# A spectral convolution whose three output blocks share one block product, with the even lags and the odd lags taken in turn

## The chip, the cores and the metric

The kernel runs on one core of a Trainium2 chip. The metric is the device time of one execution in microseconds (us), the median of the runs of a kernel. PE is the matmul engine TensorE and PEld its weight loads, DVE is VectorE, ACT is ScalarE, POOL is GpSimd and SP is SyncE, whose queue issues the loads used here.

## The reference, cut to what matters

The whole kernel is a small network of four blocks. The change touches one part, the spectral unit (`_L0_ffn_ref` in the reference). For 16 filters `phi[:, k]` of 4096 taps it makes the causal convolution of the tokens `u` with the filter and with its sign-alternated twin, and multiplies each result by a 128x128 matrix of that filter:

```
Vf = rfft(phi); Uf_p = rfft(u); Uf_m = rfft(u * sgn)
U_plus  = irfft(Vf * Uf_p)[:sl]
U_minus = irfft(Vf * Uf_m)[:sl] * sgn
out  = einsum('btkd,k,kde->bte', U_plus, sigma**0.25, Mpp)
out += einsum('btkd,k,kde->bte', U_minus, sigma**0.25, Mpm)
```

The plus and minus results are the sum and the difference of the convolution over the even lags and that over the odd lags. So the kernel computes these two instead, and mixes them with `Mpp + Mpm` and `Mpp - Mpm`. The output is added over four prefixes of the sequence, each with its own matrices and weight, which is why a mixing product is cut at 144, 288, 576 and 1152 positions.

## The kernel before, in words

Here there are 4 sequences (`B`) of 2304 tokens. Tokens are split by parity, so each sequence has 1152 (`HALF`) positions in each of two parities `q`. They are cut into 9 blocks (`GB`) of 128 for the inputs and into 3 ranges `c` (`NCW`) of 384 (`CW`) for the outputs. A causal convolution is then a lower triangular block matrix: output range `c` is a sum over the input blocks up to it. Three input blocks against one output range are a **block product**: nine matmuls of 384 columns where the lags are full, and three each of 384, 256 and 128 columns on the diagonal, where half the square is empty. There are three matmuls for each block because every operand is kept as a rounded high half and a low half, of which three of the four products are made.

`spectral_unit` normalises and transposes the tokens, `autoregress` makes a short convolution into `YT` and splits the tokens into `u_high` and `u_low`, and `convolve` does the work of this study. In `convolve`, for each filter `k` of 16 (`NK`), 24 units `(b, c, q)` are run with `c` from 2 down to 0. For a unit:

- TensorE's `conv` (L1068) makes the even lags into one bank of PSUM and the odd lags into the next: 3 block products for each kind where `c` is 2, 2 where it is 1, 1 where it is 0, one of which is the diagonal one.
- ScalarE (L1107) copies both banks as `uk_high`; VectorE (`lower`, L1163) subtracts this copy from the banks and so makes `uk_low`. Both work on 128x768.
- TensorE's `mix` (L1084), two units behind `conv`, multiplies by the matrices into bank 6 or 7, both kinds into one sum; VectorE adds it to `YT` (L1175, 128x384).

GpSimd splits the filters of the next `k` into halves (L1122, L1124: four operations of 1152 elements), kept twice. SyncE loads filters and matrices. VectorE prepares the next matrices in seven steps. The order is that of the code on each engine, held together by semaphores; TensorE's loop body (L1049) holds two filters, so it jumps back seven times. At the end of each filter TensorE waits for its own last `mix` before it releases the filters:

```
for n in range(UNITS):
    conv(n)
    if n >= 2:
        mix(n - 2)
mix(UNITS - 2)
mix(UNITS - 1)
pe.wait_ge(s["mixed"], k * UNITS + (UNITS + 3))
pe.sem_inc(s["filter_used"], 1)
```

## Time and profile before

| what | value |
|---|---|
| median of three runs | 11514.84 us (11510.84 to 11519.92) |
| the profiled execution, its device time | 11517.94 us |
| its span, first to last instruction | 11515.4 us |
| mean granted TensorE clock over the span | 0.884 |
| busy over the whole span | PE 81%, DVE 57%, ACT 38%, POOL 34% |
| `convolve`, first matmul to last addition | 4627.15 to 7406.71 us, 2779.6 us |

The shares over the whole span mix many stages. `convolve` is one of them, a quarter of the time, and its rows are read by themselves. A matmul row shows when it starts and how long it takes to the end of its pipeline; neighbours overlap, so the cost of one is the distance from its start to the next start. A row of waits says which engine stood idle, and what ended that.

### The profile page before, as it was taken

The page shows a single profiled execution, that of the slowest core. Times are in us where ns is not written, and L with a number is a line of the kernel's source. Part 1 is how long each engine was busy: PE and PEld are TensorE (multiplying, and loading weights), DVE is VectorE, ACT ScalarE, POOL GpSimd, SP SyncE. Part 2 cuts the span into 40 slices and gives each one's busy share as a digit, 9 for nine tenths or more (in the row PEclk, how much of TensorE's full clock was granted, in tenths as well). Part 3 has the DMA queues.
Part 4 walks back from the last instruction along what each step waited for, and adds up shares of the span by engine and source line. Part 5 has one row for each costly group of instructions (what it writes and reads, how often), then busy time and mean ns, then how long its engine had stood idle before and what let it go on. Part 6 is the DMA issues. An engine that isn't in the chain of part 4 may idle for free. (4 is left out here: it accounts for less than half of the span.)

```text
span 11515.4 us, 138604 instructions
## 1 busy us (share of the span) xinstructions
PE 9299.0 (81%) x45020; PEld 6323.7 (55%) x45020; DVE 6604.9 (57%) x8044; ACT 4361.7 (38%) x7821; POOL 3888.3 (34%) x2670
## 2 busy tenths in 40 slices
PE   4777777777777775999999999778748989897567
PEld 2334343333433343999999999767523333333355
DVE  6999799899979995222222222211256566652446
ACT  4666566556646664111111111122313444444221
POOL 4998699689959993100000000000000000000001
PEclk8888888898888888999999999866858999998677
DMA  3454355344535452000000000111210100001110
GB/s 124 155 159 140 123 155 159 116 147 156 158 95 167 157 157 65 25 13 7 13 13 7 13 13 1 50 45 30 118 35 20 23 17 13 17 13 63 66 27 17
DMA packets 335211, 831.37 MB, mean 72 GB/s; under 512 B 37778, under 2 KB 111894, under 8 KB 324060
## 3 DMA queue, kind: packets, MB, share of 16 engines
q1 hardware_dynamic: 334628, 823.93, 23.1%
q8 instruction: 325, 5.32, 0.2%
q14 instruction: 258, 2.11, 0.1%
HBM read 757.40 MB, written 37.82 MB: 69 GB/s over the span
## 5 line engine op out<-in xcount | busy, mean ns | idle before, releaser
L669 POOL TENSOR_TENSOR ss_work<-ss_dtu,ss_ringb 128x768 f32<-128x768 f32 x1536 | 2754.1, 1816 | 3.8
L557 PE MATMUL ss_ps<-ss_work,ss_ident 128*128 128x512 f32 (+1 forms) x6144 | 2369.2, 538 | 264.3 <-DVE ss_work L640 158.5
L557 PEld LDWEIGHTS ss_ps<-ss_work,ss_ident 128*128 128x128 f32 x6144 | 1247.2, 210 | 1165.2 <-issue 761.0
L653 DVE TENSOR_TENSOR_SCAN ss_work<-ss_ps,ss_last,ss_work 128x768 f32<-128x768 f32 x1024 | 1801.1, 1797 | 0.0
L1163 DVE TENSOR_TENSOR cv_uk_low<-cv_ps,cv_uk_high 128x768 fp32r<-128x768 f32 x384 | 367.7, 958 | 2086.8 <-ACT cv_uk_high L1107 2086.8
L582 ACT ACTIVATE ss_ps<-ss_dt,ss_a_neg 128x768 f32<-128x768 f32 x1536 | 1370.5, 892 | 174.0 <-DVE ss_work L653 166.9
L1107 ACT ACTIVATE cv_uk_high<-cv_ps 128x768 fp32r<-128x768 f32 x384 | 311.9, 812 | 2480.6 <-PE cv_ps L1068 2480.6
L640 DVE TENSOR_TENSOR ss_work<-ss_work,ss_ps 128x1280 f32<-128x1280 f32 x768 | 1126.6, 1467 | 134.2 <-ACT ss_ps L582 114.8
L2142 DVE TENSOR_REDUCE at_top<-at_ps 128x384 f32 (+1 forms) x1728 | 888.7, 551 | 259.1 <-PE at_ps L2061 258.1
L2124 ACT ACTIVATE at_probs<-at_ps 128x768 f32<-128x768 f32 x864 | 695.9, 810 | 872.1 <-PE at_ps L2078 872.1
L653 DVE TENSOR_TENSOR_SCAN ss_work<-ss_ps,ss_work 128x768 f32<-128x768 f32 x512 | 871.0, 1737 | 64.2 <-POOL ss_work L669 64.1
L1122 POOL TENSOR_TENSOR cv_even_high<-cv_even,cv_one 128x1152 fp32r<-128x1152 f32 x16 | 33.7, 2106 | 2307.2 <-PEq L1096 2294.2
L1068 PE MATMUL cv_ps<-cv_even_high,stu_u_high 128*128 128x384 f32 (+2 forms) x2304 | 737.3, 320 | 52.4 <-issue 29.7
L1543 POOL MEMSET c_pooled<- 128x2048 f32 x2 | 3.6, 1807 | 2283.5 <-POOLq L59 2283.5
L2078 PE MATMUL at_ps<-at_packs 128*128 (+1 forms) x3456 | 711.3, 332 | 76.1 <-PEq L59 58.4
L2085 PE MATMUL at_ps<-at_probs,at_v 128*64 128x384 f32 x3456 | 753.4, 515 | 15.6 <-ACT at_probs L2124 13.5
L1068 PE MATMUL cv_ps<-cv_even_low,stu_u_high 128*128 128x384 f32 (+2 forms) x2304 | 744.2, 323 | 0.0
L1068 PE MATMUL cv_ps<-cv_even_high,stu_u_low 128*128 128x384 f32 (+2 forms) x2304 | 741.2, 322 | 0.0
L529 PE MATMUL ss_ps<-ss_dtr,ss_dtw 64*128 64x192 f32 (+1 forms) x736 | 294.6, 489 | 548.3 <-DVE ss_work L640 519.6
L1068 PE MATMUL cv_ps<-cv_odd_low,stu_u_high 128*128 128x384 f32 (+2 forms) x2304 | 736.4, 320 | 0.0
L1068 PE MATMUL cv_ps<-cv_odd_high,stu_u_high 128*128 128x384 f32 (+2 forms) x2304 | 736.3, 320 | 0.0
L1068 PE MATMUL cv_ps<-cv_odd_high,stu_u_low 128*128 128x384 f32 (+2 forms) x2304 | 735.7, 319 | 0.0
(527 smaller groups left out, 15405.1 us busy)
## 6 DMA issues: line engine op xcount, KB each, us to landing
ss_ringb<-scan_rows SPq DMA_DIRECT2D x768, 384.0 KB, 3.7
ss_ringc<-scan_rows SPq DMA_DIRECT2D x768, 384.0 KB, 3.8
c_w<-in_l_ffn_w SPq DMA_DIRECT2D x64, 1024.0 KB, 7.0
at_packs<-at_parts SPq DMA_DIRECT2D x192, 144.0 KB, 3.2
cv_odd<-in_l_ffn_phi_odd SPq DMA_DIRECT2D x16, 576.5 KB, 5.7
cv_even<-in_l_ffn_phi_even SPq DMA_DIRECT2D x16, 576.0 KB, 4.1
ffa_rows<-rows SPq DMA_DIRECT2D x16, 576.0 KB, 6.3
ffb_w<-in_l_conv_fw SPq DMA_DIRECT2D x50, 128.0 KB, 2.0
```

The costliest lines, as they stand in the source:

```text
L557: ins = pe.matmul(acc[:, d * WIN + a:d * WIN + e], ident[:, :], weighed[:, t % DEEP, d, a:e], start=False, stop=n == NST - 1, skip_group_c ...
L582: act.activation(decay[d], dt[:, i % 2, d, :], ACT.Exp, scale=a_neg[:, SECTIONS[i][0], d, n:n + 1]).then_inc(s["decayed"], 1)
L640: dve.tensor_tensor(weighed[:, t % DEEP, :, 0:SPLIT], hid[:, t % DEEP, :, 0:SPLIT], bc(spread_c[:, None, :], [P, D2, SPLIT]), ALU.mult).th ...
L653: dve.tensor_tensor_scan(hid[:, t % DEEP, d, ::step], decay[d][:, ::step], drive[:, t % DEEP, d, ::step], start, ALU.mult, ALU.add).then_i ...
L669: pool.tensor_tensor(drive[:, t % DEEP, d, :], dtu[:, t // NST % 2, d, :], ringb[:, t % RING, :], ALU.mult).then_inc(s["driven"], 1)
L1068: ins = pe.matmul(ps[:, 2 * (n % 3) + kind, off:CW], (u_high, u_low)[a][:, b * GB + g, parity, :], filters[f][:, u, ::-1][:, from_:from_ + ...
L1107: act.activation(uk_high[:, n % 3, :, :], ps[:, at:at + 2, 0:CW], ACT.Copy).then_inc(s["kept"], 1)
L1163: dve.tensor_tensor(uk_low[:, n % 3, :, :], ps[:, at:at + 2, 0:CW], uk_high[:, n % 3, :, :], ALU.subtract).then_inc(s["lowered"], 1)
L2078: ins = pe.matmul(ps_bank(ps, 2 * (j % 2) + h)[:, 0:R], packs[:, pair, k, h, j * P:(j + 1) * P], packs[:, pair, q, h, bass.ds(c * R, R)], ...
L2085: ins = pe.matmul(acc[64 * h:64 * h + 64, 0:R], v[:, j, 2 * pair + h, :, :].rearrange("p a d -> p (a d)"), probs[:, j % 3, h, :], start=j ...
L2124: act.activation(probs[:, j % 3, :, :], ps[:, 2 * (j % 2):2 * (j % 2) + 2, 0:R], ACT.Exp).then_inc(s["weighed"], 1)
L2142: dve.tensor_reduce(top[:, bass.ds(tile + h * NT_, 1), u], ps_bank(ps, 5 + u % 3)[:, 0:R], AX.X, ALU.max).then_inc(s["reduced"], 1)
```

## The change

Write the block matrix with `F0` for the diagonal block of taps, `F1` and `F2` for the next ones, and `u0`, `u1`, `u2` for the three ranges of input. The outputs are `F0 u0`, `F1 u0 + F0 u1` and `F2 u0 + F1 u1 + F0 u2`: three diagonal products and three full ones. The new code makes one product `F1 (u0 + u1)` (`SHARED`), `F0 u0` (`FIRST`), `(F0 - F1) u1` (`SECOND`) and `(F2 - F1) u0 + F0 u2` (`THIRD`), and VectorE adds the shared product to the second and third output (`join`). That is two diagonal products and four bank groups with three full ones: one diagonal product fewer, five block products in place of six.

The even and the odd kind are run in turn: a filter is now 16 units (`PER`) `(kind, b, q)`, first all eight even ones. The banks are 0 to 3 for the four products and 4 to 6 for the mixing of `c` 0, 1 and 2. Each kind is mixed and added to `YT` by itself. The taps `near` (F0 and F1), `less` (F0 - F1) and `far` (F2 - F1) of a kind are kept once and made by GpSimd from one raw tile in nine operations for each kind. `autoregress` also makes the sums `u0 + u1` and splits them (`s_high`, `s_low`). TensorE's loop body holds one filter, the first filter stands ahead of the loop.

```
+            s_high, s_low = (flat[:, i * n:(i + 1) * n].rearrange("p (g t c) -> p g t c", t=2, c=C).bitcast(F32R) for i in range(2))
+            spare = flat[:, 2 * n:3 * n].rearrange("p (s t) -> p s t", t=CW).bitcast(F32R)
...
+                for b in range(B):
+                    dve.tensor_tensor(sums[:, b], U[:, b * GB:b * GB + NCW, :, :], U[:, b * GB + NCW:b * GB + 2 * NCW, :, :], ALU.add).then_inc(s["summed"], 1)
...
+                for b in range(B):
+                    dve.wait_ge(s["sum_cut"], b + 1)
+                    dve.tensor_tensor(s_low[:, b * NCW:(b + 1) * NCW, :, :], sums[:, b], s_high[:, b * NCW:(b + 1) * NCW, :, :], ALU.subtract)
...
+                    act.wait_ge(s["summed"], b + 1)
+                    act.activation(s_high[:, b * NCW:(b + 1) * NCW, :, :], sums[:, b], ACT.Copy).then_inc(s["sum_cut"], 1)
...
+    PAIRS = [(b, q) for b in range(B) for q in range(2)]
+    PER = 2 * len(PAIRS)
...
+        raw = sb("raw", [P, HALF + 1])
+        near = [[sbr(f"near{kind}{part}", [P, WIDE + kind]) for part in range(2)] for kind in range(2)]
+        less = [[sbr(f"less{kind}{part}", [P, APART + kind]) for part in range(2)] for kind in range(2)]
+        far = [[sbr(f"far{kind}{part}", [P, APART + kind]) for part in range(2)] for kind in range(2)]
+        apart = sb("apart", [P, APART + 1])
...
+        shared = sb("shared", [P, 2, CW])
...
+                with sp.Fori(0, NK) as k:
+                    sp.wait_ge(ready[1], k + 1)
+                    sp.dma_start(raw[:, 0:HALF], bass.AP(w["phi_even"].tensor, k * rows, [[1, P], [1, HALF]])).then_inc(loaded[0], 16)
...
+                    sp.wait_ge(ready[0], k + 2)
+                    sp.dma_start(raw[:, :], bass.AP(w["phi_odd"].tensor, k * rows, [[1, P], [1, HALF + 1]])).then_inc(loaded[1], 16)
...
+                        pool.wait_ge(loaded[kind], k * 16 + 16)
+                        pool.wait_ge(s["convolved"], k * (4 * PER) + 2 * PER * (kind + 1))
+                        halve(1, near[kind], taps[:, CW:HALF + kind], WIDE + kind)
+                        pool.tensor_tensor(apart[:, 0:CW + kind], taps[:, WIDE:WIDE + CW + kind], taps[:, CW:WIDE + kind], ALU.subtract).then_inc(s["split"], 1)
+                        pool.tensor_tensor(apart[:, CW + kind:more], bc(none[:, :], [P, 2 * P]), taps[:, WIDE + kind:WIDE + 2 * P + kind], ALU.subtract).then_inc(s["split"], 1)
+                        pool.wait_ge(s["split"], done + 3)
+                        halve(4, less[kind], apart[:, 0:more], more).then_inc(s["split"], 1)
+                        pool.wait_ge(s["split"], done + 5)
+                        pool.tensor_tensor(apart[:, 0:more], taps[:, 0:more], taps[:, CW:CW + more], ALU.subtract).then_inc(s["split"], 1)
+                        pool.wait_ge(s["split"], done + 6)
+                        halve(7, far[kind], apart[:, 0:more], more).then_inc(ready[kind], 1)
...
+                def product(n, bank, blocks, taps, first, narrow, start, stop):
+                    kind, b, q = unit(n)
+                    parity, shift = ((q, 0), (1 - q, q))[kind]
+                    for g in range(NCW):
+                        off = g * P if narrow else 0
+                        from_ = first + shift - (0 if narrow else g * P)
+                        for turn, (a, f) in enumerate(HI_LO):
+                            ins = pe.matmul(ps[:, bank, off:CW], blocks(a, g, parity), taps[kind][f][:, ::-1][:, from_:from_ + CW - off],
+                                            start=start and g == 0 and turn == 0, stop=stop and g == NCW - 1 and turn == 2, skip_group_check=True)
+                    return ins
...
+                    at = k * (NCW * PER) + (NCW * n + c + 1)
+                    pe.wait_ge(s["kept"], at)
+                    pe.wait_ge(s["lowered"], at + NCW)
+                    pe.wait_ge(s["added"], at)
+                    for lo, hi, seg in pieces(c):
+                        for turn, (a, f) in enumerate(HI_LO):
+                            ins = pe.matmul(ps[:, 4 + c, lo:hi], (eff_high, eff_low)[a][:, kind, seg, :], (uk_high, uk_low)[f][:, (NCW * n + c) % SLOTS, lo:hi],
+                                            start=turn == 0, stop=turn == 2, skip_group_check=True)
+                    ins.then_inc(s["mixed"], 1)
+
+                def body(k, before):
+                    for n in range(PER):
+                        kind, b, q = unit(n)
+                        if n % len(PAIRS) == 0:
+                            pe.wait_ge(ready[kind], k + 2)
+                        last = k * (NCW * PER) + NCW * n
+                        pe.wait_ge(s["shared"], k * PER + (n + 1))
+                        product(n, SHARED, lambda a, g, parity: (s_high, s_low)[a][:, b * NCW + g, parity, :], near, CW, False, True, True).then_inc(s["convolved"], 1)
+                        if n or before is not None:
+                            mix(k if n else before, n - 1 if n else PER - 1, 0)
+                        pe.wait_ge(s["lowered"], last + 1)
+                        product(n, FIRST, of(b, 0), near, 0, True, True, True).then_inc(s["convolved"], 1)
+                        if n or before is not None:
+                            mix(k if n else before, n - 1 if n else PER - 1, 1)
+                        pe.wait_ge(s["lowered"], last + 2)
+                        product(n, SECOND, of(b, 1), less, 2 * P, False, True, True).then_inc(s["convolved"], 1)
+                        if n or before is not None:
+                            mix(k if n else before, n - 1 if n else PER - 1, 2)
+                        pe.wait_ge(s["lowered"], last + 3)
+                        product(n, THIRD, of(b, 0), far, 2 * P, False, True, False)
+                        product(n, THIRD, of(b, 2), near, 0, True, False, True).then_inc(s["convolved"], 1)
+
+                pe.sem_inc(s["convolved"], 4 * PER)
+                body(0, None)
+                with pe.Fori(0, NK - 1) as i:
+                    body(i + 1, i)
...
+                        act.wait_ge(s["convolved"], made + SHARED + 1)
+                        act.wait_ge(s["joined"], k * (2 * PER) + (2 * n + 2))
+                        act.activation(shared[:, n % 2, :], ps[:, SHARED, 0:CW], ACT.Copy).then_inc(s["shared"], 1)
+                        for c in range(NCW):
+                            if c:
+                                act.wait_ge(s["joined"], k * (2 * PER) + (2 * n + c + 4))
+                            else:
+                                act.wait_ge(s["convolved"], made + FIRST + 1)
+                            act.wait_ge(s["mixed"], free + c + 1)
+                            act.activation(uk_high[:, (NCW * n + c) % SLOTS, :], ps[:, FIRST + c, 0:CW], ACT.Copy).then_inc(s["kept"], 1)
...
+                    dve.tensor_tensor(ps[:, FIRST + c, 0:CW], ps[:, FIRST + c, 0:CW], shared[:, n % 2, :], ALU.add).then_inc(s["joined"], 1)
+
+                def body(k, before, after):
+                    for n in range(PER):
+                        late = (k, n - 1) if n else (before, PER - 1)
+                        for c in range(NCW):
+                            if late[0] is not None:
+                                add(*late, c)
+                            if c:
+                                join(k, n, c)
+                            lower(k, n, c)
+                        if n in (2, 3):
+                            halve_matrices(n - 2, 1, k * (NCW * PER) + SLOTS)
+                        if after is not None and 9 <= n < 14:
+                            sum_matrices(n - 9, after)
+                        if after is not None and n >= 14:
+                            halve_matrices(n - 14, 0, k * (NCW * PER) + (SLOTS + NCW * PER // 2))
```

On TensorE, this stood in the middle of a filter before, the end of the even lags of a unit with `c` = 2 and the start of its odd lags (`stu_u_high` is the weight, `cv_even_high` the moving taps):

```order
L1068 MATMUL cv_ps<-cv_even_high,stu_u_high 128x256
L1068 MATMUL cv_ps<-cv_even_low,stu_u_high 128x256
L1068 MATMUL cv_ps<-cv_even_high,stu_u_low 128x256
L1068 MATMUL cv_ps<-cv_even_high,stu_u_high 128x128
L1068 MATMUL cv_ps<-cv_even_low,stu_u_high 128x128
L1068 MATMUL cv_ps<-cv_even_high,stu_u_low 128x128
L1068 MATMUL cv_ps<-cv_odd_high,stu_u_high 128x384
L1068 MATMUL cv_ps<-cv_odd_low,stu_u_high 128x384
L1068 MATMUL cv_ps<-cv_odd_high,stu_u_low 128x384
```

Now the first filter's second unit begins like this (`stu_XT` holds `s_high` and `s_low` in the shared product and `uk_high` and `uk_low` in the mixing one):

```order
L1103 MATMUL cv_ps<-cv_near,stu_XT 128x384 [waits cv_shared]
L1103 MATMUL cv_ps<-cv_near,stu_XT 128x384 x8
L1120 MATMUL cv_ps<-stu_XT,cv_eff_high 128x144 [waits cv_lowered,cv_added,cv_kept,cv_eff_ready]
L1120 MATMUL cv_ps<-stu_XT,cv_eff_high 128x144
L1120 MATMUL cv_ps<-stu_XT,cv_eff_low 128x144
L1120 MATMUL cv_ps<-stu_XT,cv_eff_high 128x144 x2
L1120 MATMUL cv_ps<-stu_XT,cv_eff_low 128x144
L1120 MATMUL cv_ps<-stu_XT,cv_eff_high 128x96 x2
L1120 MATMUL cv_ps<-stu_XT,cv_eff_low 128x96
L1103 MATMUL cv_ps<-cv_near,stu_u_high 128x384 [waits cv_lowered]
L1103 MATMUL cv_ps<-cv_near,stu_u_high 128x384
```

The shared product stands first in a unit, and the mixing of the unit before is spread behind the four products, one range at a time, with a wait ahead of each. A diagonal group (384, 256, 128 columns) is what there is one fewer of. At the end of TensorE's loop body the rows are these:

```order
L1103 MATMUL cv_ps<-cv_near,stu_u_low 128x128
L1148 REGISTER_ALU
L1148 COMPARE_AND_BRANCH
L1120 MATMUL cv_ps<-stu_XT,cv_eff_high 128x144 [waits cv_added,cv_lowered,cv_kept]
```

The jump stands behind each filter and no wait for TensorE's own `mix` is ahead of it; the last row is the first one after the loop.

On VectorE, in the middle of a filter before, the subtractions of 768 elements and the additions to `YT` alternate:

```order
L1163 TENSOR_TENSOR cv_uk_low<-cv_ps,cv_uk_high 128x768 [waits cv_kept]
L1175 TENSOR_TENSOR stu_YT<-stu_YT,cv_ps 128x384 [waits cv_mixed]
L1161 REGISTER_ALU
L1163 TENSOR_TENSOR cv_uk_low<-cv_ps,cv_uk_high 128x768 [waits cv_kept]
L1175 TENSOR_TENSOR stu_YT<-stu_YT,cv_ps 128x384 [waits cv_mixed]
L1161 REGISTER_ALU
L1163 TENSOR_TENSOR cv_uk_low<-cv_ps,cv_uk_high 128x768 [waits cv_kept]
```

And now (L1206 adds to `YT`, L1216 is `join`, L1210 is `lower`):

```order
L1206 TENSOR_TENSOR stu_YT<-stu_YT,cv_ps 128x384 [waits cv_mixed]
L1216 TENSOR_TENSOR cv_ps<-cv_ps,cv_shared 128x384 [waits cv_convolved,cv_shared]
L1210 TENSOR_TENSOR stu_XT<-cv_ps,stu_XT 128x384 [waits cv_kept]
L1206 TENSOR_TENSOR stu_YT<-stu_YT,cv_ps 128x384 [waits cv_mixed]
L1216 TENSOR_TENSOR cv_ps<-cv_ps,cv_shared 128x384 [waits cv_convolved]
L1210 TENSOR_TENSOR stu_XT<-cv_ps,stu_XT 128x384 [waits cv_kept]
L1206 TENSOR_TENSOR stu_YT<-stu_YT,cv_ps 128x384 [waits cv_mixed]
L1210 TENSOR_TENSOR stu_XT<-cv_ps,stu_XT 128x384 [waits cv_kept]
```

The eight rows are one unit: three additions, two joins and three subtractions, all of 384 elements. A filter has 16 such units, 128 operations; before it had 24 pairs, 48 operations. An addition, which waits for TensorE's mixing, now stands ahead of each subtraction or join, which release a bank.

## Rows read from the trace of the kernel before

**Rows 1.** Windows of two stretches: busy time and instructions by engine, granted clock, DMA share, GB/s

```profile
4650.00:4824.00 174.00, 173.50 (x1176) 173.40 (x1175) 40.16 (x61) 20.31 (x25) 9.47 (x4) 1.00 0.04 11
4824.00:4998.00 174.00, 169.59 (x1135) 169.50 (x1134) 39.23 (x60) 18.68 (x23) 9.01 (x4) 0.98 0.04 11
```

**Rows 2.** Waits from 4600 to 7420: us in total, times, longest us

```profile
ACT cv_uk_high L1107 <- PE cv_ps L1068: 2480.6, 384, 28.8
PE cv_ps L1068 <- issue: 29.7, 7, 4.4
PE cv_ps L1068 <- POOL cv_odd_low L1124: 18.7, 1, 18.7
PE cv_ps L1068 <- PE cv_ps L1084: 4.0, 8, 0.5
```

**Rows 3.** Timeline of TensorE at 5007: start us, us, what

```profile
5007.62 0.34 PE L1068 MATMUL cv_ps<-cv_even_high,stu_u_low 128*128 128x384 f32 x1
5007.79 0.28 PE L1068 MATMUL cv_ps<-cv_even_high,stu_u_high 128*128 128x256 f32 x1
...
5008.15 0.23 PE L1068 MATMUL cv_ps<-cv_even_high,stu_u_high 128*128 128x128 f32 x1
...
5008.43 0.39 PE L1068 MATMUL cv_ps<-cv_odd_high,stu_u_high 128*128 128x384 f32 x1
5008.66 0.34 PE L1068 MATMUL cv_ps<-cv_odd_low,stu_u_high 128*128 128x384 f32 x1
```

**Rows 4.** Timeline of ScalarE: first and last of seven copies

```profile
5205.16 0.81 ACT L1107 ACTIVATE cv_uk_high<-cv_ps 128x768 fp32r<-128x768 f32 x1 [10.00 <-PE cv_ps L1068]
...
5247.74 0.81 ACT L1107 ACTIVATE cv_uk_high<-cv_ps 128x768 fp32r<-128x768 f32 x1 [10.00 <-PE cv_ps L1068]
```

**Rows 5.** Timeline of GpSimd: the first operation of three filters

```profile
4798.90 2.11 POOL L1122 TENSOR_TENSOR cv_even_high<-cv_even,cv_one 128x1152 fp32r<-128x1152 f32 x1 [156.31 <-PEq L1096]
...
4969.88 2.11 POOL L1122 TENSOR_TENSOR cv_even_high<-cv_even,cv_one 128x1152 fp32r<-128x1152 f32 x1 [161.36 <-PEq L1096]
...
5146.41 2.11 POOL L1122 TENSOR_TENSOR cv_even_high<-cv_even,cv_one 128x1152 fp32r<-128x1152 f32 x1 [167.36 <-PEq L1096]
```

**Rows 6.** Timeline of TensorE where its loop jumps back

```profile
4969.43 0.28 PE L1084 MATMUL cv_ps<-cv_uk_high,cv_eff_low 128*128 128x96 f32 x1
4974.11 0.66 PE L1068 MATMUL cv_ps<-cv_even_high,stu_u_high 128*128 128x384 f32 x1 [4.41 <-issue]
...
4979.04 0.34 PE L1068 MATMUL cv_ps<-cv_even_high,stu_u_high 128*128 128x384 f32 x1
```

**Rows 7.** Groups of VectorE by line and form, 4600 to 7420

```profile
L1163 DVE TENSOR_TENSOR cv_uk_low<-cv_ps,cv_uk_high 128x768 fp32r<-128x768 f32 x384 | 367.7, 958 | 2086.8 <-ACT cv_uk_high L1107 2086.8
L1175 DVE TENSOR_TENSOR stu_YT<-stu_YT,cv_ps 128x384 f32<-128x384 f32 x384 | 210.0, 547 | 59.0 <-PE cv_ps L1084 58.8
```

**Rows 8.** Timeline around the start of the stage

```profile
4608.57 0.49 ACT L999 ACTIVATE stu_YT<-ar_ps 128x384 f32 x1 [1.45 <-PE ar_ps L987]
...
4616.53 2.11 POOL L1122 TENSOR_TENSOR cv_even_high<-cv_even,cv_one 128x1152 fp32r<-128x1152 f32 x1 [6.50 <-DMA cv_odd<-in_l_ffn_phi_odd]
...
4619.10 3.09 DVE L1141 TENSOR_TENSOR cv_mm<-cv_mp,cv_mm 128x512 f32<-128x512 f32 x1
...
4627.15 0.66 PE L1068 MATMUL cv_ps<-cv_even_high,stu_u_high 128*128 128x384 f32 x1 [18.71 <-POOL cv_odd_low L1124]
```

**Rows 9.** Timeline: VectorE while GpSimd works, some us later

```profile
4638.18 2.10 POOL L1122 TENSOR_TENSOR cv_odd_high<-cv_odd,cv_one 128x1153 fp32r<-128x1153 f32 x1
...
4638.70 0.96 DVE L1163 TENSOR_TENSOR cv_uk_low<-cv_ps,cv_uk_high 128x768 fp32r<-128x768 f32 x1 [8.09 <-ACT cv_uk_high L1107]
```

**Rows 10.** Timeline of ScalarE and VectorE at the end of the stage

```profile
7400.80 0.81 ACT L1107 ACTIVATE cv_uk_high<-cv_ps 128x768 fp32r<-128x768 f32 x1 [2.97 <-PE cv_ps L1068]
...
7406.15 0.56 DVE L1175 TENSOR_TENSOR stu_YT<-stu_YT,cv_ps 128x384 f32<-128x384 f32 x1 [1.46 <-PE cv_ps L1084]
```

**Rows 11.** Timeline of VectorE in `autoregress`

```profile
4562.56 4.96 DVE L971 TENSOR_TENSOR stu_u_low<-stu_u,stu_u_high 128x4608 fp32r<-128x4608 f32 x1 [5.45 <-ACT stu_u_high L994]
```

More of the change, by code:

```diff
@@ L1189, in convolve @@
+                ch.leave(NK - 2)
+                body(NK - 1, NK - 2, None)
+                for c in range(NCW):
+                    add(NK - 1, PER - 1, c)
         s.end()
```

245 lines of the change are left out of this document (104 added, 141 removed).

## The prediction

> **What bounds the kernel now.** I read the windows first. In a stretch of one filter TensorE is busy 173.50 of 174 us at a granted clock of 1.00, VectorE 40.16, ScalarE 20.31 and GpSimd 9.47 [rows 1]. The waits say the same from the other side: ScalarE waits for TensorE 384 times, 2480.6 us in all, while TensorE's own waits in the stage are 18.7 us for the first filters, seven of together 29.7 us put down to nothing that the profile shows, and eight of together 4.0 us for its own mixing [rows 2]. So TensorE's stream of matmuls sets the time of the stage; the other engines cost nothing until they hold it up.
>
> The price of a matmul is read from the distance of starts. Full ones of 384 columns follow each other at 0.17 to 0.18 us. A diagonal group's 256s begin at 5007.79 and its 128s at 5008.15, and the next group starts at 5008.43; the matmul after that follows at 0.23 us instead of 0.175, a price of a short group that goes to whoever stands behind it [rows 3]. One round of six units, both kinds of one `(b, q)`, is 5247.74 - 5205.16 = 42.58 us for two, 21.29 us for one [rows 4]. Eight of them are 170.3 us. Filters follow at 4969.88 - 4798.90 = 170.98 us where no loop jump lies between, and at 5146.41 - 4969.88 = 176.53 us where one does [rows 5]. The jump itself is seen: the last mixing matmul starts at 4969.43, the next at 4974.11, with 4.41 us idle for "issue", and then 15 matmuls take 4979.04 - 4974.11 = 4.93 us, 0.32 us each where 0.175 was usual [rows 6]. That is TensorE at the lower level of its clock, 1.2 GHz, after it stood still for 4.4 us. So a jump costs about 4.5 us of standing and 4.93 - 15 x 0.175 = 2.3 us of slow matmuls, 6.8 us; the two periods give 176.53 - 170.3 = 6.2 us. I take 6.5. The end of a filter without a jump costs 170.98 - 170.3 = 0.7 us, the wait for its own mixing.
>
> **TensorE's work.** For each kind and `(b, q)` one diagonal product goes: three matmuls of 384 (3 x 0.175 = 0.53 us) and six shorter ones (5008.43 - 5007.79 = 0.64 us), together 1.17 us [rows 3]. The penalty of 0.05 us behind a short group does not go, since a unit now has three places where a long group follows a short one and two old units of one kind had about as many. There are 16 filters x 8 x 2 = 256 such products: 256 x 1.17 = 299.5 us less. The mixing has the same matmuls as before, in other order. A unit of one kind is then (21.29 - 2.34) / 2 = 9.48 us, a filter 151.6 us. TensorE changes to another group with waits 14 times where it did 12 times for the same work. Such changes are hardly seen: summed from the starts a round is 21.0 us against 21.29 measured, 0.02 us a change. 2 x 0.02 x 128 = 5 us more.
>
> **The loop.** The body holds one filter, and the first filter stands ahead of the loop. 15 passes jump back 14 times, before 7. Before: 7 x 6.5 + 8 x 0.7 = 51 us. After: 14 x 6.5 = 91 us, with no wait for the own mixing. That is 40 us more. The body is 1008 matmuls with as many loads where it was 2304; if it is still fetched anew at each jump, the price of a jump stands. Bounds for a jump: nothing, if the shorter body is held (14 x 6.5 = 91 us less than I say), and twice the price, if the other engines' jumps delay the filter's beginning as well (91 us more). The Trainium skill, "Runtime: NRT & Kernel Launch", section "Instruction fetch mechanics", says that a taken branch to a target outside the sequencer's present window forces a fetch before the engine goes on, and gives TensorE's instruction memory as 2048 instructions. The rule speaks against this change, as the trace's seven stops do; by the memory's figure the new body of some 2,090 instructions is just too long to be held, and the sum stays.
>
> **The other engines.** ScalarE copied 128x768 at 0.81 us [rows 4]; 128x384 out of PSUM takes it 0.49 us [rows 8]. A unit of 9.48 us has four such copies, 2.0 us. VectorE took 0.958 us for 768 elements and 0.547 us for 384 [rows 7]; `join`, which writes PSUM, is in no row, and I bound it by 0.547 us (its count of elements) and 0.958 us (twice that) and take 0.55, since both known forms read PSUM and go by the element. Eight operations are 4.4 us, 5.2 at the upper bound, of 9.48; matrix steps add at most 1.5. In TensorE's own order, with 0 the start of a unit: the shared product ends at 1.6, the first at 3.8, the second at 6.1, the third at 9.4. ScalarE has the shared sum by 2.2. The first range is copied and lowered by 5.0, the second joined, copied and lowered by 7.9, the third by 2.0 of the next unit. TensorE wants them for mixing at 1.6, 3.8 and 6.1 of the next unit, and wants the banks again at 2.6, 4.5 and 6.6. The tightest of these is late only if it slips by 4 us or more. Behind an addition on VectorE, which waits for mixing, stand a join and a subtraction; the mixing it waits for is done before the product that they need. So all of this is hidden behind matmuls, at no cost. Where the loop jumps, ScalarE and VectorE jump too, each after its last operation, 1 to 3 us later than TensorE; TensorE's first shared product after a jump ends 7 us after the last third product, and a jump of some 4.5 us on them fits.
>
> GpSimd takes 2.11 us for 1152 elements, 1.83 ns each; at the start, beside VectorE, its four operations took 4627.15 - 4616.53 = 10.6 us for 4610 elements [rows 8]. A kind now has 5376 elements, so 10 to 12.5 us, with a load of some 6.5 us [rows 8] ahead. It has eight units, 75 us, for it. Hidden; if that cover were gone it would cost 19 us for each of 31 kinds.
>
> **The ends.** At the start GpSimd needs to wait only for the even load, up to 2 us sooner, and has up to 2 us more to do before TensorE begins: 0. In `autoregress` VectorE stands idle for 5.45 us ahead of L971 [rows 11], and the four sums of 768 elements, at 4.96 / 4608 us for one, 0.8 us each, fit there. Behind the last copy to `YT`, at 4608.57 [rows 8], ScalarE has four copies of 768 elements more and VectorE a last subtraction: 4 x 0.81 + 0.96 = 4.2 us on the path. At the end, the last copy starts at 7400.80 and the last addition at 7406.15 [rows 10], 5.9 us with it. Now two of the three mixings run while the last range is evicted: join 0.55, copy 0.49, lower 0.55, three matmuls 0.6, addition 0.55, 2.8 us with the handing over 3.2. That is 2.7 us less.
>
> **The sum.** -299.5 + 5 + 40 + 4.2 - 2.7 = -253 us. From the profiled execution's own time, 11517.94, that is 11265; the median of the three runs is 3.1 us lower, so I say 11262 us, 2.2% faster. Three runs of before lie within 9 us, under 0.1%; 0.2% (23 us) is about what can be told from no change.
>
> **The rivals.** *The jumps cost nothing.* The new body is less than half the old. For: loops of few instructions elsewhere need not be fetched. Against: 4.4 us is lost at every one of the seven old jumps [rows 2], and the new body is still over 2000 instructions with its loads. Time: 11262 - 91 = 11171. Chance 0.05.
>
> *The jumps cost twice.* ScalarE's and VectorE's bodies are longer than before in ScalarE's case (64 operations for 24), and the shared sum must be copied before the next shared product may overwrite its bank. Against: the slack of some 3 us at the jump, worked out above. Time: 11262 + 91 = 11353. Chance 0.08.
>
> *VectorE becomes the bound, slower than before.* All three evictions of a unit and its additions pass through VectorE in one fixed order, with GpSimd more than twice as busy beside it. For: with GpSimd at work VectorE took 3.09 us for 512 elements at the start [rows 8]. Against: some 20 us later a subtraction that reads PSUM took 0.96 us beside GpSimd, its usual time [rows 9], and every operation of the unit's chain reads PSUM. It decides from 9.48 us of VectorE's work in a unit, and the kernel is slower than before from 9.48 + 253 / 256 = 10.5 us, 1.3 us an operation. At 1.53 us, half of the 3.09 us row, it is 12.2 us: 256 x (12.2 - 9.48) = 700 us more, 11960. Chance 0.03.
>
> *The single filter buffers are late.* Load and splitting shown at each change of kind, 31 x 19 = 590 us more, 11850. Against: 75 us of cover. Chance 0.02.
>
> *The change does less than it says.* This cannot be by count: the code has 1008 matmuls for a filter in place of 1152. The price of what goes can be smaller: by columns alone, 3 x 768 at 0.175 / 384 us, a product is 1.05 us, and the gain 31 us less. That lies in the forecast's own range.
>
> **How the numbers follow.** The forecast has 0.82. Its own range is 11235 to 11305: the product between 1.05 us (+31) and 1.22 us with the penalty behind it (-13), the jump between 6.2 and 6.8 us (2 us either way), 10 us for the ends. For 8 in 10 I go from 11190, towards the free jumps, to 11360, which holds the doubled ones. Faster by over 0.2%: the forecast and both cases of the jump, 0.94 of their 0.95. Slower: 0.05. Within: 0.01.
>
> **What would show it.** TensorE over 99% busy between jumps, a filter at 151 to 153 us without the jump; 14 waits of 4 to 4.5 us for "issue" and none above 0.5 us for VectorE or ScalarE; `join` at 0.5 to 0.6 us; VectorE near 70 to 75 us busy in a filter, GpSimd 20 to 25; the stage at about 2522 us in place of 2779.6. The prediction is wrong if TensorE waits for `lowered`, `shared` or the filters, if its clock falls between jumps, or if the jumps' price is another.

## The result and the profile after

| | before | after |
|---|---|---|
| median of the runs | 11512.84 us (11507.78 to 11519.92, 4 runs) | 11186.64 us (11167.34 to 11189.08, 4 runs) |
| profiled execution, device time | 11517.94 us | 11187.02 us |
| stage, first matmul to last addition | 2779.6 us | 2426.7 us |
| the rest of that execution | 8738.4 us | 8760.3 us |
| mean granted clock | 0.884 | 0.881 |

The ratio is 0.9713 with a 95% interval of 0.9696 to 0.9729: 2.9% faster, where 2.2% was forecast. The time lies 3 us below the predicted range (11190 to 11360 us). The stage gave 352.9 us, and 257 were forecast for it. The rest of the program took 22 us more in this execution. Some 5 of these are the change's own, 4.5 at the longer end of `autoregress` and 0.8 between it and the first matmul; the others are what the rest varies by, since over the profiled executions of this study it lies between 8727 and 8763 us.

One filter of the changed kernel in the windows, against [rows 1] (same columns):

```profile
4866.00:5017.60 151.60, 150.62 (x1010) 150.48 (x1010) 75.15 (x142) 31.48 (x64) 24.50 (x18) 1.00 0.04 12
```

TensorE is full but for 0.98 us, in a stretch that holds a loop jump. VectorE's 75 us, ScalarE's 31 and GpSimd's 24.5 are what was forecast (70 to 75, 32, and 20 to 25). The waits of the stage, against [rows 2]:

```profile
POOL cv_near L1078 <- PE cv_ps L1103: 1887.1, 30, 63.6
ACT stu_XT L1169 <- DVE cv_ps L1216: 1331.2, 512, 2.8
ACT stu_XT L1169 <- PE cv_ps L1103: 447.9, 256, 1.8
DVE cv_ps L1216 <- PE cv_ps L1103: 446.3, 512, 1.1
PE cv_ps L1103 <- POOL cv_far L1080: 24.0, 1, 24.0
PE cv_ps L1103 <- issue: 14.0, 14, 1.3
```

No row has TensorE waiting for VectorE or ScalarE. Its fourteen jumps cost 14.0 us together, where the seven of before cost 29.7; GpSimd waits 63 us for each kind's turn, so its cover is large. The jump on TensorE, against [rows 6]:

```profile
4941.10 0.27 PE L1103 MATMUL cv_ps<-cv_near,stu_u_low 128*128 128x128 f32 x1
4942.36 1.84 PE L1103 MATMUL cv_ps<-cv_near,stu_XT 128*128 128x384 f32 x9 [0.98 <-issue]
4944.04 0.34 PE L1120 MATMUL cv_ps<-stu_XT,cv_eff_high 128*128 128x144 f32 x2
```

It stands still for 0.98 us, not 4.41, and the nine matmuls behind take 4944.04 - 4942.36 = 1.68 us, 0.187 each: the clock stays at 2.4 GHz. GpSimd's first operation of each filter, against [rows 5], gives the price:

```profile
4715.75 1.47 POOL L1078 TENSOR_TENSOR cv_near<-cv_raw,cv_one 128x768 fp32r<-128x768 f32 x1 [59.27 <-PE cv_ps L1103]
...
4866.12 1.47 POOL L1078 TENSOR_TENSOR cv_near<-cv_raw,cv_one 128x768 fp32r<-128x768 f32 x1 [62.10 <-PE cv_ps L1103]
...
5017.69 1.47 POOL L1078 TENSOR_TENSOR cv_near<-cv_raw,cv_one 128x768 fp32r<-128x768 f32 x1 [63.29 <-PE cv_ps L1103]
```

From the written-out filter into the loop there is no jump: 150.37 us, 9.40 us a unit. With one it is 151.57, and 151.4 to 151.8 over all of them. A jump costs 1.2 us. The groups of the chain, against [rows 7]:

```profile
L1210 DVE TENSOR_TENSOR stu_XT<-cv_ps,stu_XT 128x384 fp32r<-128x384 f32 x768 | 428.2, 558 | 636.8 <-ACT stu_XT L1169 636.8
L1206 DVE TENSOR_TENSOR stu_YT<-stu_YT,cv_ps 128x384 f32<-128x384 f32 x768 | 420.3, 547 | 145.3 <-PE cv_ps L1120 135.5 <-DVE cv_eff_low L1199 8.1
L1169 ACT ACTIVATE stu_XT<-cv_ps 128x384 fp32r<-128x384 f32 x768 | 377.7, 492 | 1779.1 <-DVE cv_ps L1216 1331.2 <-PE cv_ps L1103 447.9
L1216 DVE TENSOR_TENSOR cv_ps<-cv_ps,cv_shared 128x384 f32<-128x384 f32 x512 | 290.1, 567 | 446.3 <-PE cv_ps L1103 446.3
```

`join` takes 567 ns: writing PSUM costs VectorE hardly more than writing `YT`. The ends, against [rows 8, 10]:

```profile
4616.37 0.49 ACT L1010 ACTIVATE stu_YT<-ar_ps 128x384 f32 x1 [1.45 <-PE ar_ps L998]
4616.76 3.03 ACT L1013 ACTIVATE stu_XT<-ar_sums 128x768 fp32r<-128x768 f32 x4
...
4622.20 0.10 POOL L1066 MEMSET cv_one<- 128x1 f32 x1 [37.09 <-POOLq L59]
...
4627.04 1.47 POOL L1078 TENSOR_TENSOR cv_near<-cv_raw,cv_one 128x768 fp32r<-128x768 f32 x1 [4.71 <-DMA cv_raw<-in_l_ffn_phi_even]
...
4628.97 2.28 DVE L1180 TENSOR_TENSOR cv_mm<-cv_mp,cv_mm 128x512 f32<-128x512 f32 x1
```

The four copies of the sums follow the last copy to `YT`, as foreseen. At the other end the last `join` starts at 7063.75, and the last three additions end 3.2 us later:

```profile
7063.75 0.57 DVE L1216 TENSOR_TENSOR cv_ps<-cv_ps,cv_shared 128x384 f32<-128x384 f32 x1 [0.97 <-PE cv_ps L1103]
...
7065.43 1.54 DVE L1206 TENSOR_TENSOR stu_YT<-stu_YT,cv_ps 128x384 f32<-128x384 f32 x3
```

### The profile page after: what moved, and what is told of

Its sections match the earlier page's. It is cut to its first block and busy times, and to the rows that moved or that the text cites. A ratio compares the mean times of both kernels' runs of the same rounds, so it can differ in the third digit from the quotient of the medians.

```text
span 11185.2 us, 139472 instructions
## 1 busy us (share of the span) xinstructions
PE 8980.1 (80%) x42716; PEld 6002.8 (54%) x42716; DVE 7179.1 (64%) x9364; ACT 4559.6 (41%) x8465; POOL 4134.1 (37%) x2895
## 5 line engine op out<-in xcount | busy, mean ns | idle before, releaser
L1169 ACT ACTIVATE stu_XT<-cv_ps 128x384 fp32r<-128x384 f32 x768 | 377.7, 492 | 1779.1 <-DVE cv_ps L1216 1331.2
L1210 DVE TENSOR_TENSOR stu_XT<-cv_ps,stu_XT 128x384 fp32r<-128x384 f32 x768 | 428.2, 558 | 636.8 <-ACT stu_XT L1169 636.8
L1078 POOL TENSOR_TENSOR cv_near<-cv_raw,cv_one 128x768 fp32r<-128x768 f32 (+1 forms) x32 | 46.9, 1467 | 1895.6 <-PE cv_ps L1103 1887.1
L676 POOL TENSOR_TENSOR ss_work<-ss_work,ss_ringc 128x256 f32<-128x256 f32 x768 | 562.2, 732 | 239.1 <-DVE ss_work L653 229.1
L1103 PE MATMUL cv_ps<-cv_near,stu_u_high 128*128 128x384 f32 (+2 forms) x3072 | 635.0, 296 | 0.0
L529 PEld LDWEIGHTS ss_ps<-ss_dtr,ss_dtw 64*128 64x128 f32 x736 | 121.8, 205 | 860.0 <-DVE ss_work L640 769.6
L1120 PE MATMUL cv_ps<-stu_XT,cv_eff_high 128*128 128x144 f32 (+3 forms) x3072 | 577.4, 282 | 0.2 <-issue 0.2
L1216 DVE TENSOR_TENSOR cv_ps<-cv_ps,cv_shared 128x384 f32<-128x384 f32 x512 | 290.1, 567 | 446.3 <-PE cv_ps L1103 446.3
L591 ACT ACTIVATE ss_ps<-ss_ringc 128x512 f32<-128x512 f32 x768 | 461.7, 601 | 253.7 <-DVE ss_work L640 210.9
```

Source lines behind the costliest of these rows:

```text
L676: pool.tensor_tensor(weighed[:, t % DEEP, :, SPLIT:WIN], hid[:, t % DEEP, :, SPLIT:WIN], bc(ringc[:, t % RING, None, SPLIT:WIN], [P, D2, W ...
L1103: ins = pe.matmul(ps[:, bank, off:CW], blocks(a, g, parity), taps[kind][f][:, ::-1][:, from_:from_ + CW - off], start=start and g == 0 and ...
L1120: ins = pe.matmul(ps[:, 4 + c, lo:hi], (eff_high, eff_low)[a][:, kind, seg, :], (uk_high, uk_low)[f][:, (NCW * n + c) % SLOTS, lo:hi], sta ...
```

## The experiments

The question was why a jump now costs 1.2 us and not 6.5. **Theory A:** the jump still brings in code (a fetch), but TensorE issues ahead of its array, and matmuls already issued cover most of the fetch. Before, the wait for its own last mixing emptied the array first (a drain), so the whole fetch was seen, and the pause drew the clock down. **Rival B:** the shorter body is held or fetched faster. Further kernels test the price of a product, of the reordering, and the slack of VectorE. Stages are read from each kernel's profiled execution; medians of kernels that ran together stand beside the kernel before on the same chip.

**Before, without the wait.** The other engines are released by counts of `convolved` in place of `filter_used`.

```
-                        pe.wait_ge(s["mixed"], k * UNITS + (UNITS + 3))
-                        pe.sem_inc(s["filter_used"], 1)
...
-                        pool.wait_ge(s["filter_used"], k + 1)
+                        pool.wait_ge(s["convolved"], k * UNITS + 1)
```

> The kernel before, with one edit: TensorE no longer waits for its own last mixing matmul at the end of a filter; GpSimd takes the release of a filter's buffers from the count of finished convolutions instead, and VectorE has it from its waits for mixing. The loop body is as long as before (2304 matmuls). Theory A (TensorE's sequencer runs ahead of the array and reaches the jump early, so that most of the fetch behind a jump lies under matmuls that are still queued; the wait at the end of a filter took that lead away): the idle time at each of the 7 jumps falls from 4.4 us to about 1 us, the matmuls behind it keep the full clock, and the kernel takes 7 x 5.3 + 8 x 0.7 = 43 us less than before, about 11470 us. Theory B (the jump is cheap in the changed kernel because its loop body is less than half as long): the 7 jumps still cost 4.4 us of idle time and 2.3 us of slow matmuls, only some 10 us are saved, about 11502 us.

11490.99 us (9 runs), ratio to before 0.9971 (0.9961 to 0.9981); stage 2754.2, 25 us less. TensorE at one of its jumps:

```profile
4974.48 0.28 PE L1084 MATMUL cv_ps<-cv_uk_high,cv_eff_low 128*128 128x96 f32 x1
4976.72 0.41 PE L1068 MATMUL cv_ps<-cv_even_high,stu_u_high 128*128 128x384 f32 x1 [1.97 <-issue]
...
4977.95 0.52 PE L1068 MATMUL cv_ps<-cv_even_high,stu_u_high 128*128 128x384 f32 x1
4978.27 0.52 PE L1068 MATMUL cv_ps<-cv_even_low,stu_u_high 128*128 128x384 f32 x1
...
4981.15 0.34 PE L1068 MATMUL cv_ps<-cv_even_low,stu_u_high 128*128 128x384 f32 x1
```

The long body is as it was, and the idle time falls from 4.41 to 1.97 us, and to between 1.62 and 1.89 us at the six other jumps. But the clock still fell: here 1.2 us after the resume, for ten matmuls at 0.32 us (4977.95 to 4981.15), at the six others from the first matmul on, fifteen of them in 4.94 us. A filter with a jump takes 173.4 to 174.4 us against 170.35 without, so a jump still costs 3.0 to 4.1 us, 3.8 in the mean. With the wait it costs 6.3 by the same measure (176.4 to 177.0 us). So here the wait was 2.5 us of the price, all of it standing still; the slow matmuls stayed. Theory A had promised more, 43 us, than the 25 that came, and rival B, with 4.4 us idle as before, fits no better.

**After, with a wait put in** at the end of the body, for the last product of the filter.

```
+                    pe.wait_ge(s["convolved"], k * (4 * PER) + 8 * PER)
```

> The changed kernel, with one wait added: at the end of each filter TensorE waits for its own last product, ahead of the jump. The loop body keeps its length (1008 matmuls). Theory A (the lead of the sequencer hides the fetch): each of the 14 jumps shows some 4 us of idle time, the matmuls after it run at the lower level of the clock for some us, and the kernel is 14 x 5.3 = 74 us slower than the changed one, about 11261 us. Theory B (the short body makes the jump cheap): the wait costs only the emptying of the array, 15 x 0.3 = 5 us, about 11192 us.

11255.69 us (4 runs), 0.9769 (0.9753 to 0.9786); stage 2502.2, 75.5 us more. TensorE at a jump:

```profile
4931.79 0.27 PE L1103 MATMUL cv_ps<-cv_near,stu_u_low 128*128 128x128 f32 x1
4936.27 3.25 PE L1103 MATMUL cv_ps<-cv_near,stu_XT 128*128 128x384 f32 x9 [4.21 <-issue]
4939.32 0.42 PE L1120 MATMUL cv_ps<-stu_XT,cv_eff_high 128*128 128x144 f32 x2
```

With the same short body, 4.21 us of idleness and nine matmuls at 0.34 us are back. All 14 jumps stand 3.7 to 4.2 us, and filters with a jump take 155.9 to 158.4 us, 157.0 in the mean, 6.6 more than the 150.37 without wait and jump. This is the jump that I had priced at 6.5. Theory A holds; rival B had put the whole wait at 5 us. That the median comes within 7 us of my forecast for the changed kernel is in part luck: the stage is 20 us shorter than the 2522 that I had, and the rest of the program longer.

**After, two filters in TensorE's body.** Two filters stand ahead of the loop, and it jumps six times.

```
+                body(1, 0)
+                with pe.Fori(0, NK // 2 - 1) as i:
+                    body(i * 2 + 2, i * 2 + 1)
+                    body(i * 2 + 3, i * 2 + 2)
```

> The changed kernel with two filters in TensorE's loop body (2016 matmuls) and two ahead of the loop: 6 jumps in place of 14. Theory A (lead of the sequencer): a jump costs the same 1.2 us, so 8 x 1.2 = 10 us less, about 11177 us, hardly to be told from the changed kernel. Theory B (length of the body): the jumps get dear again, 6 x 6.5 - 14 x 1.2 = 22 us more, about 11209 us, with idle times near 4 us at the jumps.

11165.58 us (4 runs), 0.9696 (0.968 to 0.9712); stage 2416.8, 9.9 us less. Each of the six jumps costs what the fourteen did:

```profile
PE cv_ps L1103 <- issue: 5.9, 6, 1.3
```

A body of 2016 matmuls jumps as cheaply as one of 1008. Rival B is out between these lengths; that of before is 2304.

**The fetch itself** can be seen in the DMA view of the same traces. The code comes in packets of 16384 bytes on queue 8. In the kernel without any jump of TensorE (its loop written out, below) they follow each other at 16 to 21 us through the stage, though the other engines still jump there. At each jump of TensorE further ones come between. These are the DMA rows of three views of 8 us in 40 slices of 0.2 us, each of which begins 3.0 us ahead of the start of the last matmul before the jump, which is thus at the border of the 15th and the 16th slice. The kernels are the changed one (4938.10 to 4946.10), before without the wait (4971.48 to 4979.48) and the changed one with a wait (4928.79 to 4936.79):

```profile
GB/s 0 0 0 0 0 0 0 82 0 0 0 0 0 0 0 0 0 0 0 0 0 0 0 82 0 0 0 0 0 0 0 0 0 0 0 0 0 0 0 0
GB/s 0 0 0 0 0 0 0 0 0 0 0 82 0 0 0 0 0 0 0 0 0 0 0 0 0 0 0 0 0 82 0 0 0 0 0 0 0 0 0 0
GB/s 0 0 0 0 0 0 0 0 0 0 0 0 0 0 0 0 0 0 0 0 0 0 82 0 0 0 0 0 0 0 0 0 0 0 0 0 0 0 0 82
```

Over all jumps of five kernels, by the packets' starts:

| kernel | matmuls in the body | jumps | packet against the start of the last matmul | from the packet to the first matmul behind | idle |
|---|---|---|---|---|---|
| changed | 1008 | 14 | 1.4 to 1.6 us ahead | 2.6 to 3.0 us | 0.8 to 1.3 us |
| two filters in the body | 2016 | 6 | 1.0 to 1.6 us ahead | 2.6 to 2.8 us | 0.8 to 1.3 us |
| before, without the wait | 2304 | 7 | 0.7 to 0.8 us ahead | 2.7 to 3.0 us | 1.6 to 2.0 us |
| changed, with a wait | 1008 | 14 | 1.3 to 1.9 us behind | 2.6 to 3.1 us | 3.7 to 4.2 us |
| before | 2304 | 7 | 1.5 to 1.7 us behind | 2.7 to 3.1 us | 4.0 to 4.4 us |

From the packet's start to the first matmul it takes 2.6 to 3.1 us everywhere, whatever the length of the body. What differs is how much of it lies behind matmuls that are still running, and that is theory A.

**The `FIRST` product twice,** the second making over the first.

```
+                        product(n, FIRST, of(b, 0), near, 0, True, True, True)
```

> The changed kernel with the diagonal product FIRST made twice in each unit, the second time over the first (the result is the same): 256 diagonal products more, which prices by itself what the change removed 256 times. By the sum of the prediction, 1.17 us each, it is 300 us slower than the changed kernel, about 11486 us; by the filter periods of the two profiles, (21.29 - 2 x 9.40) / 2 = 1.245 us each, 319 us, about 11506 us. If the other engines were near to being the bound in the changed kernel, the extra TensorE time would be partly covered and cost less than 280 us.

11481.6 us (8 runs), 0.9969 (0.9959 to 0.998); stage 2737.9, 311.2 us more. By GpSimd's starts a filter without a jump takes 4883.82 - 4714.01 = 169.81 us against 150.37, 19.4 us for 16 products, 1.21 us each. I had 1.17.

**The sharing undone,** all else kept: no `SHARED` product, no `join`; the second range is made of two products in its bank and the third of three. This kernel does the block products of before in the order of after.

```
-                        product(n, SHARED, lambda a, g, parity: (s_high, s_low)[a][:, b * NCW + g, parity, :], near, CW, False, True, True).then_inc(s["convolved"], 1)
+                        product(n, SECOND, of(b, 0), near, CW, False, True, False).then_inc(s["convolved"], 1)
...
+                        product(n, THIRD, of(b, 1), near, CW, False, False, False)
```

> The changed kernel with the sharing undone and the rest kept: kinds in turn, filters kept once, the same order of mixing, the cheap jump. The second output is made as F1 u0 + F0 u1 and the third as F2 u0 + F1 u1 + F0 u2 in their own banks; ScalarE makes no shared copy and VectorE no join (48 copies and 96 operations of 384 elements a filter stay). TensorE has the 1152 matmuls a filter of the kernel before. If the whole gain is TensorE's removed diagonal products, this is 256 x 1.21 = 309 us slower than the changed kernel, about 11490 us, and some 20 to 30 us faster than before, which is the cheap jump and the end of the wait. Rival: the eviction chain of copy, join and subtraction holds TensorE up a little in the changed kernel; then removing the joins gives some of it back and the kernel is under 11470 us.

11484.21 us (10 runs), 0.9971 (0.9962 to 0.9981); stage 2738.1. The sharing is worth 2738.1 - 2426.7 = 311 us, 1.22 us a product. The reordering alone, without the wait for its own mixing, is worth 2779.6 - 2738.1 = 41 us, where I had booked a loss of 45. A filter without a jump takes 169.76 us here and 170.35 in before without the wait: 16 x 0.59 = 9 us are the new order of the matmuls, and nearly all of the other 32 the jumps and the wait.

**More work on VectorE:** one, two or three more operations of 384 elements, which read the bank, ahead of every subtraction. The first:

```
+                    ch.link(dve.tensor_tensor(scratch[:, :], ps[:, FIRST + c, 0:CW], uk_high[:, (NCW * n + c) % SLOTS, :], ALU.subtract))
```

> The changed kernel with one more VectorE operation of 128x384 (from PSUM into an unused tile) ahead of each subtraction, and a wait for it: 3 x 0.56 us more in each unit, VectorE's work goes from 4.7 to 6.5 us of 9.4, and each range is lowered some 0.65 us later. The prediction's slack of 4 us says: no cost, within 20 us of the changed kernel. The rival that VectorE's chain is near to being the bound says: up to 3 x 0.65 x 256 = 500 us more.

11176.03 us (4 runs), 0.9709 (0.9693 to 0.9725); stage 2428.7, 2 us more: hidden.

> The same with three such operations ahead of each subtraction: 9 x 0.6 = 5.4 us more in a unit, VectorE's work is 10.1 us where TensorE's unit is 9.4. If VectorE bounds only where its work in a unit exceeds TensorE's, as the prediction had it, the stage is (10.1 - 9.4) x 256 = 180 us slower, between 100 and 300 us, about 11370 us, with TensorE waiting for VectorE for a short time in each unit. If the length of the chain decides instead, it is slower by 500 us or more, with TensorE's clock falling.

11624.23 us (4 runs), 1.0098 (1.0081 to 1.0115), 1% slower than before; stage 2871.8, 445 us more than the changed kernel's. That is far more than the 180 that busy time gave, and less than the 500 or more with a falling clock that I had written beside it; the clock stays at 0.99. Yet VectorE isn't full; windows of the kernel with three:

```profile
5200.00:5700.00 500.00, 442.55 (x2822) 425.43 (x2822) 417.34 (x802) 78.36 (x179) 60.86 (x45) 0.99 0.03 9
```

Its timeline shows what holds it, one range from addition to addition:

```profile
5185.79 0.54 DVE L1207 TENSOR_TENSOR stu_YT<-stu_YT,cv_ps 128x384 f32<-128x384 f32 x1
5186.25 0.56 DVE L1220 TENSOR_TENSOR cv_ps<-cv_ps,cv_shared 128x384 f32<-128x384 f32 x1
5187.44 0.56 DVE L1211 TENSOR_TENSOR cv_scratch<-cv_ps,stu_XT 128x384 f32<-128x384 f32 x1 [0.64 <-ACT stu_XT L1170]
...
5189.70 0.54 DVE L1207 TENSOR_TENSOR stu_YT<-stu_YT,cv_ps 128x384 f32<-128x384 f32 x1
```

Behind each `join` VectorE stands 0.64 us until ScalarE has copied the range, and dependent operations follow at 0.59 us where they last 0.56. These gaps are not busy time, but they are in the cycle: 3.91 us for this range, 180.1 us for a filter, 11.26 for a unit (the first of a unit's three ranges has no `join`). TensorE now waits for VectorE:

```profile
PE cv_ps L1121 <- DVE stu_XT L1214: 294.7, 268, 3.4
```

The kernel with two tells the chain from the busy time:

> Two more VectorE operations of 384 elements ahead of every subtraction. Theory by chain: VectorE's unit is 48 x 0.59 / 16 = 1.77 us shorter than the 11.26 us with three, 9.49 us, just above TensorE's 9.40: a filter of 151.8 us instead of 150.4 to 151.5, and 5 to 30 us more than the changed kernel, with first short waits of TensorE's mixing for the subtraction. Theory by busy time: VectorE is busy 334.6 + 83 = 418 of 500 us, far from full, and the stage stays at 2427 us within 3 us.

11177.5 us (4 runs), 0.9704 (0.9689 to 0.9719); stage 2435.3, 8.6 us more, filters with a jump at 152.1 to 152.4 us in place of 151.5, and first short waits of TensorE for the subtraction, with VectorE busy 401.9 of 500 us. The chain had it right. The third operation then cost 180.1 - 152.1 = 28.0 us a filter, its full 48 x 0.59 = 28.3.

**No jump at all:** TensorE's loop written out, the other engines' kept; and, beside it, the kernel with two filters in its body and the changed kernel once more.

```
-                with pe.Fori(0, NK - 1) as i:
+                for i in range(NK - 1):
```

> The changed kernel with TensorE's loop over the filters written out, so that it jumps at no place in the stage; the other engines keep their loops. Theory A (a jump costs TensorE only its fetch, 1.0 us idle or 1.2 us of period, as long as TensorE issues ahead): 14 x 1.2 = 17 us less than the changed kernel, a stage of 2426.7 - 17 = 2410 us, every filter at 150.4 us, no wait put down to issue. Rival: the code has to be brought in for straight code as well, and without a loop each of the 16 filters is new code that comes at the speed of the fetch; then TensorE stands still in the middle of filters, and the stage is at or above 2427 us. Rival: the other engines' jumps are what TensorE waits for; then filters stay at 151.5 us and the idle 1 us is put down to them.

> The changed kernel with two filters in TensorE's body and 6 jumps, a second time, beside the changed kernel itself: a stage 8 x 1.2 = 10 us shorter, 2417 us, and a median 10 us below that of the changed kernel, less than what the part outside the stage varies by (15 us) between executions.

> The changed kernel again, to be read beside the two other kernels of this set: a stage of 2427 us, a median between 11167 and 11190 us.

| kernel | median | ratio to before | stage | rest |
|---|---|---|---|---|
| written out | 11142.33 us (5 runs) | 0.9675 (0.9662 to 0.9688) | 2409.7 us | 8727.5 us |
| two in a body | 11171.17 us (5 runs) | 0.9692 (0.9679 to 0.9705) | 2418.0 us | 8759.1 us |
| changed kernel | 11175.56 us (5 runs) | 0.9699 (0.9686 to 0.9712) | 2427.2 us | 8753.3 us |

Written out, the stage is 17.5 us shorter, every filter from the second on takes 150.37 us (4853.32 to 5003.70 to 5154.07 on GpSimd), and the window is full:

```profile
5200.00:5700.00 500.00, 500.00 (x3354) 500.00 (x3353) 250.56 (x474) 104.21 (x213) 85.85 (x63) 1.00 0.04 13
```

That is 14 x 1.2 us, so the other engines' jumps cost TensorE nothing, and fresh code in a straight line comes in time. This is the fastest of the kernels measured. Of its 33 us over the changed kernel 17.5 are the stage's; the others fall outside it. One stretch of 100 us, 500 us behind the end of the stage, shows how the rest can differ, here in the written-out kernel

```profile
7537.05:7637.05 100.00, 93.11 (x506) 86.48 (x506) 16.87 (x20) 33.06 (x47) 2.33 (x1) 0.62 0.00 0
```

and here in the changed one that ran beside it:

```profile
7557.30:7657.30 100.00, 93.69 (x424) 87.51 (x425) 14.08 (x17) 29.78 (x40) 3.22 (x1) 0.52 0.00 0
```

At a granted clock of 0.62 TensorE gets 506 matmuls done, at 0.52 only 424. In another execution of the same changed kernel the same stretch (7566.34 to 7666.34, in the set with the sharing undone) has 0.65 and 455 matmuls, so the grant varies from execution to execution of one kernel. Why the rest of the program is shorter in the written-out kernel stays open.

**The changed kernel a second time,** with the kernels of the sharing:

> The changed kernel once more, unchanged, so that the two versions near it are compared on the same chip, and to see how much of the time outside the stage differs between executions: the stage is expected at 2427 us again, the rest between 8738 and 8761 us.

11171.21 us (4 runs), 0.9704 (0.9688 to 0.972), stage 2427.3. Three sets of the same kernel give medians of 11186.64, 11171.21 and 11175.56 with the same stage within 0.6 us; the 15 us between sets are the rest of the program.

## Why the prediction was right in its direction and wrong in its size

**What bounds the kernel, and the other engines.** Right. TensorE stayed the bound, `join` cost 0.567 us, VectorE, ScalarE and GpSimd stood where they were put, and no row has TensorE waiting for them behind the first filters.

**TensorE's work.** The mechanism was right, the size a little off: 256 products at 1.21 to 1.22 us are worth 309 to 311 us, not 299.5. The 0.05 us behind a short group, which I let stand as not saved, would make up the difference. The new order of the matmuls, booked as a loss of 5 us, is a gain of 9. A filter without wait and jump came down from 170.35 to 150.37 us, 320 us for 16, where 294.5 were booked: 25 us more.

**The loop: the step that failed.** "if it is still fetched anew at each jump, the price of a jump stands" is false. The code is fetched anew at each jump, and the price doesn't stand. The price of 6.5 us belonged to a jump behind a drained engine, and the same code ended that wait: I wrote "with no wait for the own mixing" in the same step, saved 0.7 us each for it, and didn't see that it was also what laid the fetch bare. Fourteen jumps cost 14 x 1.2 = 17 us, not 91: 74 us of the stage's 95.7 us that I missed. The matmuls' 25 are the rest; the two make 99, and the old loops (49 us by the filters' periods, not 51) and the ends take some 3 back. The kernel with the wait put back returns 75.5 us. Against before, the loops are a gain of about 32 us (49 to 17), not a loss of 40. Only a part of that step is the wait alone: taking it out of the kernel before brought its jump from 6.3 to 3.8 us, and the last 2.6 came with the rest of the change: the packet starts 1.5 us ahead of the last matmul in place of 0.75, and the shorter pause leaves the clock up. Of the signs of being wrong that I had written down this is the last one, "if the jumps' price is another".

**The rivals.** *The jumps cost nothing* gave 11171 us, and three sets gave 11171 to 11187, so its number was nearly right. That is luck: the jumps' 17 us and the matmuls' 25 nearly cancel. Its reason, a body short enough to be held, fell with the body of two filters, with the wait put back and with the packet at every jump. I had tied the cheap jump to that one mechanism and so gave it 0.05. *Twice the price* and *late filter buffers* didn't occur. *VectorE becomes the bound* is real, but its point was reckoned wrongly: by work of 9.48 us a unit, when the waits for ScalarE within the cycle count too. By the series, two more operations in each range (16 x 3 x 2 x 0.59 = 57 us a filter, 3.5 a unit) just pass TensorE's pace. So, as an estimate, VectorE's cycle has 3.5 us of slack in a unit, and its eight operations could each be 0.4 us longer, 1.0 us, before TensorE feels it; I had it at 1.2.

**The ends.** `autoregress` ends 4.5 us later in its chain (4.2 booked), counted from its last copy to `YT` to GpSimd's memset. The end of the stage takes 3.2 us as worked out, and the start, from the memset to the first matmul, takes 18.0 us against 17.2 (0 booked).

**The Trainium skill's rule** on taken branches ("Runtime: NRT & Kernel Launch", "Instruction fetch mechanics"), that a target outside the present window forces a fetch, agrees with the trace. The DMA view of the changed kernel from 4936 to 4950, around the jump, has on queue 8 (packets, MB, share)

```profile
q8 instruction: 3, 0.05, 1.3%
```

and over the 56 us ahead of it three packets too, so code keeps coming, with a burst at the jump. The 74 us lay in how much of that fetch passes behind matmuls already issued.

**What stays open.** Why the kernel before, without the wait, still pauses 1.6 to 2.0 us at a jump, where the changed one pauses 0.8 to 1.3: its packet starts later against its last matmul, and its last matmuls ahead of the jump are short ones of the mixing. An estimate from the starts fits that: if TensorE is some 18 matmuls ahead, these last 1.9 us there and 2.6 us in the changed kernel, and with the distance to the next start both come to 3.7 to 4.2 us. The 18 is fitted, and no run varied what stands ahead of the jump. Nor does a run tell why the clock falls behind the one kind of pause and not behind the other, or whether the pause alone decides it.

## What to carry to other kernels

A stop that the profile puts down to "issue" at a loop jump has a price only together with what stands ahead of it: look whether the engine waits for its own last result there, and price the jump without that wait as a case of its own. Before a drain is put or left at the end of a body, count it as the whole fetch and the slow clock behind it: here 5.4 us a jump in the changed kernel (75.5 / 14), and 2.5 in the kernel before, where the fetch was covered less. By the packets and the estimate above, what stands last in a body matters too: the time that the matmuls issued ahead take is the cover. And where an engine's operations alternate with another engine's in one order, find the point where it becomes the bound from the whole cycle, waits included, not from its busy time.

## What the runs showed of the hardware

- A jump of TensorE's loop: 0.8 to 1.3 us idle where matmuls of 384 to 128 columns stand ahead of it (bodies of 1008 and of 2016 matmuls alike), 1.6 to 2.0 us where matmuls of 144 and 96 columns do, 3.7 to 4.4 us with the engine drained. In each case the first matmul behind the jump starts 2.6 to 3.1 us after a packet of code.
- VectorE's operations of 128x128 elements in SBUF took 1.36 to 1.69 us beside GpSimd's at the start (4632.79 to 4637.30) and 0.34 us without (5203.23, kernel with two more operations), while those that read PSUM kept their time beside it (4648.58, 0.56 us; its mean over the stage is 0.558).
- After 0.98 us of idleness the matmuls go on at 2.4 GHz (0.187 us for 384 columns, the clock at 1.00), and so after all 14 pauses of 0.8 to 1.3 us (fifteen matmuls in 2.30 to 2.34 us); after 4.2 us nine follow at 0.34 us each, 1.2 GHz (the clock at 0.50). After six pauses of 1.62 to 1.89 us the first fifteen took 4.94 us, at 1.2 GHz (the clock at 0.50 from 5320.2 to 5325.0); after one of 1.97 us the clock fell only 1.2 us past the resume, for ten matmuls.
- Straight code of 16 x 1008 matmuls ran with no stop that the trace shows: 500.00 us busy of 500.
- VectorE writing PSUM from PSUM takes 567 ns for 128x384, 547 ns for the addition to `YT`.
